# Four graph layers on one core: receiver rows gathered by GpSimd in part of the second sweep, run lengths for ranks, transfers split at a multiple of 16

## The reference

```python
edge_index = jnp.stack([src, dst])
x = _layernorm(x + _L0_gnn_ref(x, edge_weight, src, dst, ...))   # max over relu([h[src], h[dst], w] W1 + b1) W2 + b2
x = _layernorm(x + _L1_gnn_ref(x, L1_gnn_factors, src, dst, ...)) # sum over relu([variables[src], factors[dst]] Wm + bm), by src
x = _layernorm(x + _L2_gnn_ref(x, edge_index, ...))               # attention, 4 heads, softmax over the edges of a receiver
x = _layernorm(x + _L3_gnn_ref(x, ...))                           # two rounds of mean aggregation
```

## Time and profile before

| | before |
|---|---|
| median of 3 runs | 5681.93 us (5680.7 to 5690.96) |
| the profiled execution | 5663.14 us, span 5661.4 us |
| PE busy | 3112.8 us (55%) |
| DVE busy | 2254.2 us (40%) |
| ACT busy | 1224.2 us (22%) |
| POOL busy | 3637.8 us (64%) |
| mean granted TensorE clock | 0.712 |
| DMA | 1015.34 MB, mean 179 GB/s |

### The profile page before, as it was taken

The page is one execution under the profiler, slowest core; times in us unless marked ns, Lnnn a source line. Parts: engine busy times, 40 slices in busy tenths (PEclk is TensorE's granted clock), DMA queues, the critical chain, the costliest instruction groups (busy, mean ns, idle before and its releaser), DMA issues. The chain is left out here.

```text
span 5661.4 us, 75437 instructions
## 1 busy us (share of the span) xinstructions
PE 3112.8 (55%) x16332; PEld 2315.0 (41%) x16332; DVE 2254.2 (40%) x4035; ACT 1224.2 (22%) x2253; POOL 3637.8 (64%) x3813
## 2 busy tenths in 40 slices
PE   1368888887488885455454533333333533333345
PEld 0345555554366664344453432333333323333333
DVE  2124444444477763455554563222222222222224
ACT  0112222222144442222232321111111211111111
POOL 3277777776601105777777766777777777777776
PEclk9579999998799997777777765555555655555557
DMA  6879999998299984334343433444444334444443
GB/s 232 307 230 303 304 304 300 300 305 276 86 311 326 326 305 89 96 104 112 102 114 102 112 96 113 129 135 127 136 128 134 115 124 135 129 135 127 136 128 104
DMA packets 693883, 1015.34 MB, mean 179 GB/s; under 512 B 145813, under 2 KB 395258, under 8 KB 683722
## 3 DMA queue, kind: packets, MB, share of 16 engines
q1 hardware_dynamic: 372248, 485.42, 25.9%
q0 software_dynamic: 134688, 301.60, 20.4%
q10 hardware_dynamic: 186780, 226.46, 11.1%
HBM read 580.47 MB, written 433.03 MB: 179 GB/s over the span
## 5 line engine op out<-in xcount | busy, mean ns | idle before, releaser
L1359 POOL DMA_INDIRECT gath<-sender_table,src_cols x1664 | 1569.9, 943 | 574.0 <-issue 504.4
L1399 PE MATMUL bank<-ident,gath 128*128 128x128 f32 x1664 | 464.1, 434 | 1277.7 <-DMA gath<-sender_table,src_cols 1277.7
L1632 POOL DMA_INDIRECT gath<-attention_table,src_cols x832 | 809.4, 973 | 262.9 <-issue 190.5
L1156 POOL DMA_INDIRECT gath<-joint_table,src_cols x832 | 788.6, 948 | 261.5 <-issue 188.3
L1399 PEld LDWEIGHTS bank<-ident,gath 128*128 128x128 f32 x1664 | 297.7, 217 | 1443.7 <-DMA gath<-sender_table,src_cols 1443.7
L1425 ACT ACTIVATE rows<-bank 128x512 f32<-128x512 f32 x416 | 248.1, 597 | 1849.5 <-PE bank L1409 1849.5
L784 POOL DMA_INDIRECT gath<-scan_rows,end_i x147 | 140.5, 955 | 569.7 <-ACTq L1559 525.8
L1331 DVE TENSOR_TENSOR_SCAN scan<-meta,scan,bank 128x512 f32<-128x512 bf16 x208 | 266.2, 1280 | 372.1 <-DVEq L1328 360.9
L1442 DVE TENSOR_TENSOR_SCAN scan<-over_head,den,bank 128x512 f32<-128x512 bf16 x104 | 133.1, 1280 | 480.7 <-PE bank L1399 480.7
L1442 DVE TENSOR_TENSOR_SCAN den<-over_head,scan,bank 128x512 f32<-128x512 bf16 x104 | 133.1, 1280 | 421.2 <-PE bank L1399 421.2
L1895 DVE TENSOR_TENSOR_SCAN scan<-bank,scan,hid 128x512 f32<-128x512 f32 x208 | 266.3, 1280 | 79.3 <-DVEq L1894 75.6
(11 more groups left out here) (269 smaller groups left out, 5907.3 us busy)
## 6 DMA issues: line engine op xcount, KB each, us to landing
scan_rows<-rows SPq DMA_DIRECT2D x624, 256.0 KB
recv<-receiver_rows SPq DMA_DIRECT2D x416, 256.0 KB
attention_scan_rows<-rows ACTq DMA_DIRECT2D x208, 264.0 KB
receiver_rows<-gath ACTq DMA_DIRECT2D x26, 2048.0 KB, 17.4
factor_rows<-gath ACTq DMA_DIRECT2D x208, 256.0 KB
scan_rows<-rows ACTq DMA_DIRECT2D x208, 256.0 KB
gath<-factor_rows SPq DMA_DIRECT2D x208, 256.0 KB
over_head<-edge_meta SPq DMA_DIRECT2D x52, 1024.0 KB
```

The lines of the kernel that those rows point to most:

```text
L1156: pool.indirect_dma_start(out=landed[s][:, c, 0:width], out_offset=None, in_=table[:, :], in_offset=bass.IndirectOffsetOnAxis(ap=src_cols[ ...
L1359: pool.indirect_dma_start(out=gath[s][:, c, 0:F], out_offset=None, in_=table[:, :], in_offset=bass.IndirectOffsetOnAxis(ap=src_cols[:, t:t ...
L1399: ins = pe.transpose(b[:, c * P:(c + 1) * P], gath[s][:, c, 0:F], ident[:, :])
L1632: pool.indirect_dma_start(out=gath[s][:, c, :], out_offset=None, in_=att_d[:, :], in_offset=bass.IndirectOffsetOnAxis(ap=src_cols[:, t:t + ...
```

## The change

- *Transfers of 103, 104 or 106 rows* are split in two, at row 96 (`EVEN`). The loads of `dst` come all before those of `src`. `START_TURN` is 6 instead of 8.
- *Run lengths for ranks.* The receiver row stands at the last edge of a run (`close_i`, `last_dst`) instead of the first. VectorE keeps for each edge the run's length so far if the edge is a last one of its run or tile, else -1 (`span_cols`). `same` is then `ahead <= span`, with `ahead` one constant tile (the distance between two edges, or over 800 where it would be negative). The rank table in memory, its loads in both sweeps and their waits go.
- *Picks in sweep 2.* For blocks 1, 4 and 6 of each eight up to block 182 (`PICKED`, 69 blocks) SyncE doesn't load `receiver_rows`. GpSimd gathers four tiles from `receiver_table` into one of the two `prod` buffers by `pick_cols`, which is the receiver's number at last edges and beyond the bound elsewhere; such rows are to be skipped and keep what was in them. TensorE waits for the landing, GpSimd for the pick before last to be used. GpSimd's node gathers come behind all picks.
- *Loops of sweep 2* are written out on SyncE, TensorE and ScalarE; VectorE's stays.
- *Node phase 3*: the four scalings of a group go from VectorE to ScalarE (`scaled_rows`), and four products of the head sums become one instruction.
- *Node phase 0*: the clearing of `scan_rows` is issued at group 4 of 13 instead of behind all stores.

```diff
+EVEN = PP // 16 * 16
+assert T % TQ == 0 and 96 == EVEN < PP <= P
...
-START_TURN = 8
+START_TURN = 6
+NOT_LAST = 8192
+PICKED = [b < NB - 24 and b % 8 in (1, 4, 6) for b in range(NB)]
+assert NR * P <= NOT_LAST
...
-        rank_d = dram("edge_rank", [1, EP], U8)
...
-                    for r, t in ((dst_r, a["dst"]), (src_r, a["src"])):
-                        sp.dma_start(flat(r)[0:PP - 1, :], t[0:E - left].rearrange("(p k) -> p k", k=run)).then_inc(loaded, 16)
-                        sp.dma_start(flat(r)[PP - 1:PP, 0:left], t[E - left:E].rearrange("(p k) -> p k", p=1)).then_inc(loaded, 16)
+                    for lo, hi in ((0, EVEN), (EVEN, PP - 1)):
+                        sp.dma_start(flat(dst_r)[lo:hi, :], a["dst"][lo * run:hi * run].rearrange("(p k) -> p k", k=run)).then_inc(loaded, 16)
+                    sp.dma_start(flat(dst_r)[PP - 1:PP, 0:left], a["dst"][E - left:E].rearrange("(p k) -> p k", p=1)).then_inc(loaded, 16)
                     with nc.allow_non_contiguous_dma("one word of each tile"):
-                        sp.dma_start(prev_r[1:PP, :], a["dst"][0:E - left].rearrange("(p k) -> p k", k=run)[:, run - 1:run]).then_inc(loaded, 16)
+                        for lo, hi in ((0, EVEN), (EVEN, PP - 1)):
...
+                            sp.dma_start(prev_r[lo + 1:hi + 1, :], a["dst"][lo * run:hi * run].rearrange("(p k) -> p k", k=run)[:, run - 1:run]).then_inc(loaded, 16)
+                    for lo, hi in ((0, EVEN), (EVEN, PP - 1)):
+                        sp.dma_start(flat(src_r)[lo:hi, :], a["src"][lo * run:hi * run].rearrange("(p k) -> p k", k=run)).then_inc(loaded, 16)
...
+                    chain(v.tensor_scalar(before_k[:, :], ahead[:, :], 0.0, 1000.0, ALU.is_lt, ALU.mult))
+                    chain(v.tensor_tensor(ahead[:, :], ahead[:, :], before_k[:, :], ALU.add))
+                    v.wait_ge(loaded, 16 * 8)
...
+                    chain(v.tensor_tensor_scan(flat(span_f)[0:PP, :], flat(begins)[0:PP, :], flat(begins)[0:PP, :], 0.0, ALU.mult, ALU.add))
+                    chain(v.tensor_scalar(flat(ends)[0:PP, 0:run - 1], flat(begins)[0:PP, 1:run], -1.0, 1.0, ALU.mult, ALU.add))
+                    chain(v.memset(ends[0:PP, :, P - 1:P], 1.0))
+                    chain(v.tensor_tensor(begins[0:PP, :, :], span_f[0:PP, :, :], count_k[0:PP, :].unsqueeze(1).to_broadcast([PP, TQ, P]), ALU.is_equal))
                     chain(v.tensor_tensor(begins[0:PP, :, :], begins[0:PP, :, :], goes[0:PP, :, 0:1].to_broadcast([PP, TQ, P]), ALU.mult))
+                    v.scalar_tensor_tensor(flat(dst_m)[0:PP, :], flat(dst_f)[0:PP, :], -float(NOT_LAST), flat(ends)[0:PP, :], ALU.add, ALU.mult).then_inc(v_done, 1)
+                    v.scalar_tensor_tensor(flat(span_f)[0:PP, :], flat(span_f)[0:PP, :], 1.0, flat(ends)[0:PP, :], ALU.add, ALU.mult).then_inc(v_done, 1)
+                    v.wait_ge(v_done, 2)
+                    v.sem_inc(v_done, -2)
+                    chain(v.tensor_scalar(flat(span_f)[0:PP, :], flat(span_f)[0:PP, :], -1.0, None, ALU.add))
                     chain(v.tensor_scalar(flat(first_b)[0:PP, :], flat(begins)[0:PP, :], -1.0, BIG, ALU.add, ALU.mult))
                     chain(v.tensor_copy(lasts_b[0:PP, :], first_b[0:PP, :, P - 1]))
...
+                        pe.transpose(bank[c % 2][:, 2 * P:2 * P + PP], dst_m[0:PP, c, :], ident[0:PP, 0:PP])
+                        pe.transpose(bank[c % 2][:, P:P + PP], span_f[0:PP, c, :], ident[0:PP, 0:PP]).then_inc(turned, 1)
...
-                                                out_offset=bass.IndirectOffsetOnAxis(ap=start_i[:, t:t + 1], axis=0),
+                                                out_offset=bass.IndirectOffsetOnAxis(ap=(start_i if k == 2 else close_i)[:, t:t + 1], axis=0),
...
+                def clear_scan(q, s):
+                    if 2 * q + s == NG // 3:
+                        sp.dma_start(scan_d[EP - CLEARED[1] * EB:EP, :].rearrange("(p r) f -> p r f", p=P),
+                                     zero_c[:, :].unsqueeze(1).to_broadcast([P, CLEARED[1] * CT, F])).then_inc(cleared, 16)
...
-                        for c in range(w):
-                            ins = v.tensor_tensor(o[:, c, :].rearrange("p (h d) -> p h d", h=HEADS), from_rows[:, c, :].rearrange("p (h d) -> p h d", h=HEADS),
-                                                  h[:, c, :].unsqueeze(2).to_broadcast([P, HEADS, HID]), ALU.mult)
-                            ins.then_inc(v_done, 1)
-                        v.wait_ge(v_done, w)
-                        v.sem_inc(v_done, -w)
+                        chain(v.tensor_tensor(o.rearrange("p c (h d) -> p c h d", h=HEADS), from_rows.rearrange("p c (h d) -> p c h d", h=HEADS),
+                                              h.unsqueeze(3).to_broadcast([P, w, HEADS, HID]), ALU.mult))
...
+                            v.wait_ge(n_y_free, 1)
+                            v.sem_inc(n_y_free, -1)
...
+                    if k == 3:
+                        chain(v.reciprocal(scale[s][:, 0:w], std[s][:, 0:w]))
+                        v.scalar_tensor_tensor(shift[s][:, 0:w], mv[s][:, 0:w, 0], -1.0, scale[s][:, 0:w], ALU.mult, ALU.mult).then_inc(n_scale, 1)
+                        return
...
+                def scaled_rows(q, s):
+                    w = GROUP_TILES[2 * q + s]
+                    x, y = x_nm[:, tiles(q, s), :], y_nm[s][:, 0:w, :]
+
+                    act.wait_ge(n_scale, 1)
+                    act.sem_inc(n_scale, -1)
+                    for c in range(w):
+                        act.activation(x[:, c, :], y[:, c, :], ACT.Identity, bias=shift[s][:, c:c + 1], scale=scale[s][:, c:c + 1]).then_inc(a_done, 1)
+                    act.wait_ge(a_done, w)
+                    act.sem_inc(a_done, -w)
+                    act.sem_inc(n_x, 1)
+                    act.sem_inc(n_tab, 1)
+                    if 2 * q + s + 2 < NG:
+                        act.sem_inc(n_y_free, 1)
...
+            picked = [prod[h][:, :].rearrange("p (c f) -> p c f", f=F) for h in range(2)]
+            turn_of = [sum(PICKED[:b]) for b in range(NB)]
...
+                pool.wait_ge(over_made, 1)
+                for b in range(NB):
+                    if not PICKED[b]:
+                        continue
+                    if turn_of[b] >= 2:
+
+                        pool.wait_ge(r_pick_free, turn_of[b] - 1)
+                    for c in range(CT):
+                        pool.indirect_dma_start(out=picked[turn_of[b] % 2][:, c, :], out_offset=None, in_=recv_d[:, :],
+                                                in_offset=bass.IndirectOffsetOnAxis(ap=pick_cols[:, b * CT + c:b * CT + c + 1], axis=0),
+                                                bounds_check=NR * P - 1, oob_is_err=False).then_inc(r_pick_in[turn_of[b] % 2], 16)
...
-                    sp.dma_start(recv[s][:, :, :], first_d[part(q, s, SLOTS, EB), :].rearrange("(p c) f -> p c f", c=CT)).then_inc(recv_in[s], 16)
+                    if not PICKED[q * SLOTS + s]:
+                        sp.dma_start(recv[s][:, :, :], first_d[part(q, s, SLOTS, EB), :].rearrange("(p c) f -> p c f", c=CT)).then_inc(recv_in[s], 16)
                     sp.dma_start(factor[s][:, :, :], factor_rows_d[part(q, s, SLOTS, EB), :].rearrange("(p c) f -> p c f", c=CT)).then_inc(recv_in[s], 16)
...
-                steps(sp, NB, SLOTS, (0, load), (7, store))
+                straight(NB, SLOTS, (0, load), (7, store))
...
+                    i = q * SLOTS + s
+                    rows_in = recv[s]
+                    if PICKED[i]:
+                        rows_in = picked[turn_of[i] % 2]
+
+                        pe.wait_ge(r_pick_in[turn_of[i] % 2], 16 * CT * (turn_of[i] // 2 + 1))
                     for c in range(CT):
                         o = b[:, c * P:(c + 1) * P]
                         pe.matmul(o, factor[s][:, c, :], ident[:, :], start=True, stop=False, is_transpose=True)
-                        ins = pe.matmul(o, recv[s][:, c, :], same_ring[s][:, c, :], start=False, stop=True)
+                        ins = pe.matmul(o, rows_in[:, c, :], same_ring[s][:, c, :], start=False, stop=True)
                     ins.then_inc(e_pre, 1)
...
-                steps(pe, NB, SLOTS, (0, go_row), (0, senders), (2, turn_back))
+                straight(NB, SLOTS, (0, go_row), (0, senders), (2, turn_back))
...
+                    if PICKED[q * SLOTS + s]:
+                        act.sem_inc(r_pick_free, 1)
...
-                steps(act, NB, SLOTS, (0, hidden), (2, keep_rows))
+                straight(NB, SLOTS, (0, hidden), (2, keep_rows))
...
 
                 def same_receiver(q, s):
 
-                    if s % 2 == 0:
-                        v.wait_ge(rank_in[s // 2], 16)
-                        v.sem_inc(rank_in[s // 2], -16)
                     v.wait_ge(e_same_free, 1)
                     v.sem_inc(e_same_free, -1)
-                    v.tensor_tensor(same_ring[s][:, :, :], rank[s][:, :].rearrange("p (c e) -> p c e", e=P),
```

(3 more changed lines are left out.)

178 lines of the change are left out of this document (92 added, 86 removed).

## The result

| | before | changed |
|---|---|---|
| median (runs) | 5681.32 us (4: 5678.27 to 5690.96) | 5608.19 us (4: 5603.39 to 5611.46) |
| ratio, 95% interval | | 0.9868 (0.9851 to 0.9885) |
| profiled execution | 5663.14, span 5661.4 | 5610.31, span 5608.4 |
| POOL busy | 3637.8 (64%) | 3944.9 (70%) |
| DMA | 1015.34 MB, 179 GB/s | 972.01 MB, 173 GB/s |

The change makes the kernel 1.3% faster, by 73 us of the medians. The two profiled executions differ by 53 only. So the stages are set out for both pairs; each column is the changed kernel's stretch less that of the kernel before, from the first and last starts of the gathers and scans in the trace.

The account below looks back on a forecast made before the run. No single bound: DMA work at the start, GpSimd's gathers in sweep 1, VectorE's sequence in sweep 2, VectorE in node phase 3. Terms -46 + 0 - 11 - 15 = -72 against the 5682 median gave 5610 us, range 5572 to 5656.

Parts of the forecast that it names:

- Start, -46: Start block: even transfers spread over the engines end it 46 us earlier; ends -54 and -30.
- the smaller of the two limits: Start: ScalarE resuming 54 us earlier, or DMA work letting the block end 46 earlier; the smaller counts.
- Earlier clearing, 0 with +4 as an end: Node phase 0: clearing `scan_rows` earlier gains 0; ends -2 and +4, as it can hold a scatter.
- the edge costs that anyway: Edge after node phase 0: GpSimd idles 8.3 us there and 9.5 at the next, where nothing is cleared late.
- Sweep 1, 0: Sweep 1: GpSimd's gathers, one each 1.25 us, are the bound, so relieving other engines or DMA gains 0.
- Sweep 2, -11: Sweep 2: shorter gaps -11, scattered late loads -3, first picks +3; together -11, ends -15 and +5.
- The gather ... hidden: Sweep 2: 12 GpSimd gathers take 15.0 us per 8 blocks, which last 21, so they cost nothing.
- Node phase 3, -15: Node phase 3: VectorE saves 1.3 us a group for 12 groups, -15; ends -18 and -8.
- No split: Start: splitting brings nothing, loads only queued behind the fills; the -46 falls away, 5656 us; chance 0.08.
- DMA bounds sweep 2: Sweep 2: DMA was the bound, so the gain is 77 in place of 14, 5547 us; chance 0.07.
- Rows not skipped: Sweep 2 picks: skipped rows are moved, 64 KB a gather; VectorE still rules, 5612 to 5620 us; chance 0.05.
- Late picks: Sweep 2: picks land late; +38 gives 5648, at worst 5700 us; chance 0.06 slower, 0.04 just cancelling.

Follow-up runs that it names:

- both pairs: Unedited kernel before and changed kernel, profiled in the study and again on one chip; the second pair measured 5674.4 (one run) and 5598.0 us.
- `one_piece_loads`: Changed kernel with the loads of dst, prev_r and src in one piece of 103 rows again: 5650.59 us.
- `no_picks`: Changed kernel with no block picked, SyncE loading receiver_rows for all 208 blocks in sweep 2: 5587.6 us.

## Why the prediction was right, and where it was not

- **Start, -46: right.** -47.0 and -48.7. The first cast at 24.3 (24 forecast), the last table store at 197.86 (198), and it was the smaller of the two limits. Undoing only the split cost 52.6 us. Undoing it moved the first scatter by 51.4; the other edits of the start cost some 3. Of the two rules of the Trainium skill, page "DMA: Bandwidth & Descriptors", the one in "Rules for kernel authors" against two transfers to partition halves doesn't carry over to 103 rows cut into 96 and 7, since by it the term was 0; the one on the engine count in "Why a DMA increments its semaphore by 16 and not by 1" agrees with the share of 0.09 that came back, of which SyncE's queue had one engine's 6.1%.
- **Earlier clearing, 0 with +4 as an end: the worse end came.** The step "the edge costs that anyway" was half wrong: 2.7 of the 8.3 were the clearing's. The other half, that it can hold a scatter, was named but priced at nothing; it cost 7.
- **Sweep 1, 0: right for GpSimd's pitch, incomplete for the end.** "GpSimd is the bound; what the change takes elsewhere is worth nothing" left out that the sweep ends with its last scan, not with its last gather. In the profile of before this distance was 16.3 and looked like a pipeline's length; in another execution it was 27.7.
- **Sweep 2, -11: right in sign, half the size.** The shorter sequence of VectorE gave what it should: 16 blocks fell from 42.64 to 41.71 without picks, 12 us a sweep (-11 forecast), late scans 2 (-3 forecast), the start +3 (+3). No run separates the rank waits from the three loops written out; that the time went from the distances with a rank wait (2.63 to 2.54, 2.97 to 2.85) speaks for the waits. What failed is "The gather ... hidden": in the steady part the picks cost 5 us more. The forecast of the share, 0.77, failed too: it took the share in proportion to the bytes, and it was 0.88.
- **Node phase 3, -15: right**, -16.6 and -15.7; the period was 4.58, 0.2 under the forecast. The forecast left 0.68 of the old 1.78 between the reciprocal and the sum (0.33 and 0.35); it is 0.47. The product's 0.2 came as priced, 0.90 to 0.69.
- **Rivals.** No split: refuted by `one_piece_loads`. DMA bounds sweep 2: refuted by `no_picks`, 0.96 and yet faster. Rows not skipped: refuted by the bytes of GpSimd's queue, and the 34 rows a block were right. Late picks: there in a small size only; TensorE waited for `prod` for 3.4 us in all, in 2 places, and picks cost 8.6 us, where this rival had 38 to 90.
- **The sum.** The medians differ by 73 and 72 in the two comparisons of the changed kernel, and 72 was forecast; but that is partly luck. The stretches with a term, start to sweep 2 without sweep 1, and node phase 3, sum to -63.1 and -66.9 in the two pairs, since node phase 0 and sweep 2 came out 3 to 6 worse each. Sweep 1's backlog, which wasn't in the forecast, fills the gap in executions where some of it is left at the end; two executions don't tell how often that is. The step "19 above it, and I forecast against that" had used the spread without knowing what it was; part of it may be this backlog.

## What to carry to other kernels

Before work is moved to a free engine to relieve a busy resource, ask whether that resource sets the pace: a share of 0.94 did not, repeating gaps on VectorE did, and the cheapest gain was a wait and a loop's edge on that engine. Look at the row count of small loads at the program's start, and split a large background transfer into pieces of the size of its neighbours. And a sweep whose bound runs at an even pitch can still end late: measure the distance from the bound's last instruction to the last result, in more than one execution.

## What was not expected of the hardware

- A second load of 128 KB (1 KB to each of 128 partitions) added 5.3 us of one engine's time to its queue, or 12.4 when it read the addresses that the next load in the queue read too; in sweep 1 the two kernels differed by 87 us.
- The DMA share doesn't follow the bytes: 321 GB/s at 0.94, 272 at 0.88, 307 at 0.96, 315 at 0.97.
- A gather with a bound keeps its packets (32 for 128 rows) when some 119 of the rows are skipped, each of which still moves 4 B, and costs GpSimd 1.00 us either way. Gathers without the bound took 0.945 in sweeps 4 and 5, with rows of the same size; that the bound makes the 0.05 is not shown.
- One issue behind a transfer of 4 MB in 512 B pieces held a queue for 15.0 us; with pieces of 256 KB, two at a time, the issue behind them took 1.26 at most.
